# Moving the finishing of a head's output from VectorE to ScalarE and GpSimd (layer 1), and the splitting of the negated maximum from VectorE to GpSimd (layers 2 and 3)

## What is computed

```
# layer 1
dots = jnp.einsum('bhid,bhjd->bhij', q, k) * scale
attn = jax.nn.softmax(dots, axis=-1)
out = jnp.einsum('bhij,bhjd->bhid', attn, v)
out = out.transpose(0, 2, 1, 3).reshape(b, n, h * d)
return out @ Wo + bo
# layers 2 and 3
attn = jnp.einsum('bhqd,bhkd->bhqk', q, k) * SCALE
attn = jax.nn.softmax(attn, axis=-1)
out = jnp.einsum('bhqk,bhkd->bhqd', attn, v)
```

## Time and profile before

| | |
|---|---|
| median of 3 runs | 5328.83 us (5327.84 to 5330.45) |
| the profiled execution | 5331.11 us, of which the span of the trace is 5329.4 us |
| layer 1's attention in the trace | about 390 to 2880 us |
| layer 2's and layer 3's attention | about 3062 to 4100 us, 4255 to 5296 us |
| busy over the span | PE 92%, DVE 86%, ACT 58%, POOL 29% |

### The profile page before, as it was taken

The page is one execution under the profiler, slowest core; times in us unless marked ns, Lnnn a source line. Parts: engine busy times, 40 slices in busy tenths (PEclk is TensorE's granted clock), DMA queues, the critical chain, the costliest instruction groups (busy, mean ns, idle before and its releaser), DMA issues. The chain is left out here.

```text
span 5329.4 us, 73754 instructions
## 1 busy us (share of the span) xinstructions
PE 4899.8 (92%) x26357; PEld 1887.1 (35%) x26366; DVE 4600.4 (86%) x4742; ACT 3093.5 (58%) x6047; POOL 1543.5 (29%) x1202
## 2 busy tenths in 40 slices
PE   8938999999999999999997599999998699999997
PEld 5623454544445454444543222222222322222222
DVE  7649989899898989989895699999996499999996
ACT  3313444444444444444443288888886188888885
POOL 0014656565565656556564100000000100000000
PEclk9968999999999999999998699999998699999998
DMA  0024334232333423233220211111110211111110
GB/s 36 5 93 111 95 85 116 57 113 54 96 88 88 111 61 114 57 90 85 57 50 15 71 28 32 31 28 28 34 23 3 72 27 34 29 28 33 30 23 6
DMA packets 171366, 298.03 MB, mean 56 GB/s; under 512 B 39060, under 2 KB 108576, under 8 KB 167392
## 3 DMA queue, kind: packets, MB, share of 16 engines
q1 hardware_dynamic: 169420, 292.95, 21.8%
q10 hardware_dynamic: 1584, 0.37, 0.0%
HBM read 187.39 MB, written 101.25 MB: 54 GB/s over the span
## 5 line engine op out<-in xcount | busy, mean ns | idle before, releaser
L1777 DVE TENSOR_REDUCE a_mx<-ps 128x1 f32<-128x1024 f32 x1536 | 1814.5, 1220 | 72.5 <-PE ps L1611 56.4
L1719 ACT ACTIVATE a_prob<-ps 128x512 f32<-128x512 f32 (+1 forms) x3264 | 1699.4, 602 | 295.8 <-PE ps L1599 290.9
L1067 ACT ACTIVATE prob<-ps 128x512 f32<-128x512 f32 (+1 forms) x1888 | 974.8, 603 | 1183.1 <-PE ps L952 1178.7
L1170 POOL TENSOR_TENSOR tot_p<-tot_p,prob 128x512 f32<-128x512 f32 (+1 forms) x896 | 1341.5, 1497 | 915.7 <-ACT prob L1067 851.0
L1095 DVE TENSOR_REDUCE mx<-ps 128x1 f32<-128x1024 f32 x896 | 1051.3, 1215 | 152.2 <-PE ps L929 144.6
L1611 PE MATMUL ps<-a_K,a_Q 59*128 59x512 bf16 (+1 forms) x3328 | 1094.3, 386 | 57.4 <-DMA a_Q<-q_stack_dram 45.3
L1118 DVE TENSOR_TENSOR tot_d<-tot_d,prob 128x512 f32<-128x512 f32 x928 | 1051.9, 1134 | 88.0 <-ACT prob L1067 36.3
L1599 PE MATMUL ps<-a_Q,a_K 59*128 59x512 bf16 (+1 forms) x3264 | 991.2, 384 | 55.1 <-ACT a_prob L1719 48.9
L963 PE MATMUL ps<-prob,V 128*64 128x512 f32 x3776 | 929.4, 605 | 0.0
L1635 PE MATMUL ps<-a_prob,a_V 128*9 128x512 f32 x6528 | 873.9, 597 | 10.9 <-ACT a_acc L1703 10.9
L951 PE MATMUL ps<-QA,KA 128*128 128x512 f32 (+1 forms) x1888 | 805.9, 427 | 0.0
(11 more groups left out here) (405 smaller groups left out, 2968.1 us busy)
## 6 DMA issues: line engine op xcount, KB each, us to landing
a_K<-k_stack_dram SPq DMA_DIRECT2D x128, 300.2 KB
k_hi_dram<-hi_s SPq DMA_DIRECT2D x112, 256.0 KB
k_lo_dram<-lo_s SPq DMA_DIRECT2D x112, 256.0 KB
KA<-k_hi_dram SPq DMA_DIRECT2D x64, 384.0 KB, 4.3
KA<-k_lo_dram SPq DMA_DIRECT2D x64, 384.0 KB, 5.6
KB<-k_hi_dram SPq DMA_DIRECT2D x64, 384.0 KB, 6.5
k_bf_dram<-bf_s SPq DMA_DIRECT2D x112, 128.0 KB
KM<-k_bf_dram SPq DMA_DIRECT2D x32, 448.0 KB, 7.1
```

Of the source, the lines that this page charges most:

```text
L1067: nc.scalar.activation(prob[0:r, batch % 2, t % BATCH, :], c.banks(n % 3)[0:r, :], ACT.Exp, scale=SCALE).then_inc(exped, 1)
L1170: nc.gpsimd.tensor_tensor(tot_p[0:r, u % 2, :], tot_p[0:r, u % 2, :], p, ALU.add).then_inc(totalled_p, 1)
L1719: nc.scalar.activation(prob[0:r, batch % 2, t % BATCH, :], c.banks(n % 3)[0:r, :], ACT.Exp, scale=SCALE).then_inc(exped, 1)
L1777: nc.vector.tensor_reduce(mx[:, u % 2, j, i % FULL:i % FULL + 1], c.banks(slot(step), 2), AX.X, ALU.max).then_inc(maxed, 1)
```

## The change

Layer 1: ACT, behind the four exponentials of batch 1, copies the sums (to `den`) and the 128x512 product (to `fin_s`) out of PSUM; the second copy frees the slot, so a "fin" slot is now counted under `v_out`. DVE keeps only the reciprocal, from `den`. POOL, behind its two sums of batch 1, multiplies `fin_s` by the reciprocals and adds it to `c.y`, two instructions of 128x512. To make room, `gain` and `shift` are given back after the norm. Layers 2 and 3: DVE keeps the reduce to the negated maximum; POOL does the cast and the subtraction.

```diff
-        by_act, count = kind == "v", [0, 0] if not freed else list(freed[-1])
+        by_act, count = kind in ("v", "fin"), [0, 0] if not freed else list(freed[-1])
...
+                def take_fin(u):
+                    n = slot_no["fin", u]
+                    act.wait_ge(slotted, n + 1)
+                    if u >= 1:
+                        act.wait_ge(added, 2 * u)
+                        act.wait_ge(rec_ready, u)
+                    nc.scalar.copy(den[:], c.banks(slot(n) + 1)[:, 0:UQ]).then_inc(fin_out, 1)
+                    nc.scalar.copy(fin_s[:], c.banks(slot(n))).then_inc(v_out, 1)
...
-                def finish(u):
-                    n = slot_no["fin", u]
-                    dve.wait_ge(slotted, n + 1)
-                    inv, f = rec[:, u % 2, :], u % HALVES
-                    link(nc.vector.reciprocal(inv, c.banks(slot(n) + 1)[:, 0:UQ]))
-                    for j in range(UQ):
-                        y = c.y[:, UQ * f + j, :]
-                        last = nc.vector.scalar_tensor_tensor(out=y, in0=c.banks(slot(n))[:, j * P:(j + 1) * P],
-                                                              scalar=inv[:, j:j + 1], in1=y, op0=ALU.mult, op1=ALU.add)
-                    last.then_inc(released, 1)
+                def invert(u):
+                    dve.wait_ge(fin_out, u + 1)
+                    if u >= 2:
+                        dve.wait_ge(added, 2 * (u - 1))
+                    nc.vector.reciprocal(rec[:, u % 2, :], den[:]).then_inc(rec_ready, 1)
...
+                def add_up(u):
+                    pool.wait_ge(rec_ready, u + 1)
+                    pool.wait_ge(v_out, freed[slot_no["fin", u]][1])
+                    if u >= 2:
+                        pool.wait_ge(added, 2 * (u - 1))
+                    y = c.y[:, UQ * (u % HALVES):UQ * (u % HALVES + 1), :]
+                    share = fin_s[:].rearrange("p (j d) -> p j d", j=UQ)
+                    nc.gpsimd.tensor_tensor(share, share, rec[:, u % 2, :].unsqueeze(2).to_broadcast([P, UQ, D]),
+                                            ALU.mult).then_inc(added, 1)
+                    pool.wait_ge(added, 2 * u + 1)
+                    nc.gpsimd.tensor_tensor(y, y, share, ALU.add).then_inc(added, 1)
...
+            @block.gpsimd
+            def _(pool):
+                for u in range(UNITS):
+                    both, hi, lo = nm[:, u % 2, :], nmp[:, u % 2, :, 0], nmp[:, u % 2, :, 1]
+                    pool.wait_ge(nm_max, u + 1)
+                    if u >= 2:
+                        pool.wait_ge(scored, nm_no(u - 2) + 1)
+                    nc.gpsimd.tensor_copy(hi, both).then_inc(nm_cut, 1)
+                    pool.wait_ge(nm_cut, u + 1)
+                    nc.gpsimd.tensor_tensor(lo, both, hi, ALU.subtract).then_inc(nm_ready, 1)
...
-                        dve.wait_ge(scored, nm_no(u - 2) + 1)
-                    link(nc.vector.tensor_reduce(nm[:, u % 2, :], mx[:, u % 2, :, :], AX.X, ALU.max, negate=True))
-                    link(nc.vector.tensor_copy(nmp[:, u % 2, :, 0], nm[:, u % 2, :]))
-                    nc.vector.tensor_tensor(nmp[:, u % 2, :, 1], nm[:, u % 2, :], nmp[:, u % 2, :, 0], ALU.subtract
-                                            ).then_inc(nm_ready, 1)
+                        dve.wait_ge(nm_ready, u - 1)
+                    nc.vector.tensor_reduce(nm[:, u % 2, :], mx[:, u % 2, :, :], AX.X, ALU.max, negate=True
+                                            ).then_inc(nm_max, 1)
```

More of the change, by code:

```diff
@@ L739, in l1_attention @@
         sb = lambda n, s, d=FP32: c.sb(n, s, d, held)
-        gain, shift, bo = sb("gain", [P, D]), sb("shift", [P, D]), sb("bo1", [P, D])
+        bo = sb("bo1", [P, D])
         weights = [sb(f"weights{i}", [P, 4, P]) for i in range(2)]
@@ L755, in l1_attention @@
         nm, rec = sb("nm1", [P, 2, UQ]), sb("rec1", [P, 2, UQ])
[L756 to L782, removed]
@@ L783, in l1_attention, with _ @@
-        norm(c, gain, shift)
+        with ExitStack() as early:
+            gain, shift = (c.sb(n, [P, D], FP32, early) for n in ("gain", "shift"))
+            with phase(nc, "loaded") as (block, loaded):
+                @block.sync
+                def _(sp):
+                    sp.dma_start(gain[:], w["ln_g"].partition_broadcast(P)).then_inc(loaded, 16)
+                    sp.dma_start(shift[:], w["ln_b"].partition_broadcast(P)).then_inc(loaded, 16)
+                    sp.dma_start(bo[:], w["bo"].partition_broadcast(P)).then_inc(loaded, 16)
+                    for base in (0, DH):
+                        sp.dma_start(Wo_twice[0][base:base + DH, :], w["Wo"][0:DH, :]).then_inc(loaded, 16)
+                    sp.wait_ge(loaded, 16 * 9)
+                @block.scalar
+                def _(act):
+                    act.dma_start(weights[0][:, W_Q, :], w["Wq"][:, 0:P]).then_inc(loaded, 16)
+                    act.dma_start(weights[0][:, W_K, :], w["Wkv"][:, 0:P]).then_inc(loaded, 16)
+                    act.dma_start(weights[0][:, W_V, :], w["Wkv"][:, HEADS * DH:HEADS * DH + P]).then_inc(loaded, 16)
+                    act.dma_start(weights[0][:, W_M, :], w["Wm"][:, 0:P]).then_inc(loaded, 16)
+                @block.vector
+                def _(dve):
+                    nc.vector.memset(ones_col[:], 1.0)
+                    nc.vector.memset(V[:, TILES - 1, :], 0.0)
+                    for tile in QB:
+                        nc.vector.memset(f32(tile[DH:P, :]), 0.0)
+                @block.gpsimd
+                def _(pool):
+                    nc.gpsimd.memset(f32(KB[DH:P, :]), 1.0)
+            norm(c, gain, shift)
@@ L1073, in _ @@
                             take_v(*what)
+                        if kind == "fin":
+                            take_fin(what)
                         if b == NM_AT and u + 1 < UNITS:
@@ L1078, in _ @@
                 take_acc(UNITS - 1)
+                take_fin(UNITS - 1)
             @block.vector
@@ L1148, in _ @@
                         if kind == "fin":
-                            finish(what)
-                finish(UNITS - 1)
+                            invert(what)
+                invert(UNITS - 1)
             @block.gpsimd
@@ L1185, in _ @@
                             cast(what)
+                        if kind == "fin":
+                            add_up(what)
+                add_up(UNITS - 1)
         with phase(nc, "chain", "unused") as (block, chain, _):
```

16 lines of the change are left out of this document (10 added, 6 removed).

## The result

The changed kernel took 5302.11 us (median of 5 runs, 5298.47 to 5304.35), the kernel before 5327.84 (5 runs, 5325.39 to 5330.45): a ratio of 0.9951, with a 95% interval of 0.9936 to 0.9965. It is faster by 25.7 us. The prediction was 5297, in a range of 5290 to 5312.

The account below looks back on a forecast made before the run. Layer 1 was taken as held up by PE waiting for DVE's finishing adds, layers 2 and 3 as paced by PE, three score banks and ACT. -33.6 + 2.3 - 0.4 = -31.7 us gave 5297.1 us, range 5290 to 5312.

Parts of the forecast that it names:

- The wait in layer 1: Layer 1: PE's wait for the finishing slot in 23 places goes, with 0.6 us from seven other units; 33.6 us gained.
- The sum: Whole kernel: -33.6 + 2.3 - 0.4 = -31.7 us, giving a median of 5297.1 us.
- DVE may run 1.4 us later against PE than it does before PE notices.: Layer 1, plain batch: PE's second pair needs its slot about 909.3, DVE freed it at 907.93, so there is room.
- the return of nothing: Layer 1: none of the time gained in batch 1 is given back later in the unit; taken as nothing.
- POOL's added work: Layer 1: two more POOL instructions, 2.6 us a unit, cost nothing as POOL has time and hardly meets DVE's sums.
- Rival (b): Layer 1: POOL holds up DVE and PE waits for DVE later; 18 us come back, 5315 us; chance 0.07.
- The tail: End of layer 1: the last finishing, with nothing to hide it, takes 3.7 us instead of 1.4; +2.3 us.
- Layers 2 and 3: Layers 2 and 3: 62 of 64 units gain nothing; only the filling of each layer gains, 0.4 us for both together.
- rival (d): Layers 2 and 3: POOL's small instructions late; from 2.1 us on every us costs 62 us, 5353 at 3; chance 0.04.
- DVE runs beside it with a little to spare: Layers 2 and 3: PE, three score banks and ACT set the pace; DVE is outside that loop with slight room.
- The forecast's own range: Whole kernel, rivals left out: 26 to 33 us gained, 5296 to 5303 us; the forecast's chance 0.80.

Follow-up runs that it names:

- experiments 4 and 5: Kernel before; in 4 DVE does layer 1's finishing ahead of its two sums, 5317.51 us; in 5 ACT copies the slot out, DVE adds from the copy, 5320.64 us.
- experiment 9: Layer 1's half of the change, ACT copying and POOL adding, but the slot freed only by DVE's reciprocal behind its two sums: 5302.49 us, ratio 0.9951.
- experiment 1: Only layer 1's half of the change, layers 2 and 3 as in the kernel before: 5297.34 us, ratio 0.9946.
- experiment 6: Layer 1's half of the change alone, with POOL adding the share once more and taking it off again in each finishing: 5316.09 us, ratio 0.998.
- experiment 3: Kernel before, with DVE doing the cast and subtraction of the negated maximum twice in layers 2 and 3: 5356.82 us, ratio 1.0057.
- experiment 10: Layer 1's half of the change, with only the last unit finished by DVE from PSUM as before: 5299.5 us, ratio 0.9945.
- experiment 11: The whole changed kernel measured once more on the same chip: 5304.48 us, ratio 0.995.
- Experiment 2: Kernel before with only the half in layers 2 and 3, the split on POOL, layer 1 untouched: 5327.62 us, ratio 1.0001.

## Why the prediction was right, and where it was not

**The wait in layer 1 (-33.6).** The mechanism was right. Layer 1 became 31.3 us shorter. The sum had 1.43 us for each of 23 places; batch 1 of a unit got shorter by 1.46 to 1.48 in 14 of them, by 1.37 to 1.39 in three and by 1.13 in six (units 3, 7, 19, 23, 27 and 29). With the seven places that open a pair of heads, which gave 0.08 each, as predicted, that is 32.0 us of 33.6. In those six, and only there, DVE's opening copy was held up by POOL, as the last section shows; DVE's maxima of batch 1 then start 0.24 us later, and so do PE's finishing products, which wait for the slot that the first of them frees. Another 0.08 us came back in batch 4 of the seven units 1, 5, ..., 25, where PE waits for L1102, 0.6 in all.

**"DVE may run 1.4 us later against PE than it does before PE notices."** This step failed. It was read off one plain batch, where PE's second pair needs a slot freed a batch earlier. It holds for batches like that one and for those of unit 3, and not for all plain ones: late in units 2, 6 and so on DVE is 1.4 us later already, and under 0.5 us is left. A batch with a projection of kind "k" asks for one slot more, and there the room is close to nothing: with DVE 1.4 us later against PE, in experiments 4 and 5, 1.40 to 1.47 us came back in batch 4 wherever that batch has such a projection. So the reason given for the return of nothing was wrong in part, and that nothing came back but 0.6 us was partly luck. What keeps the gain is the other half of the same argument, the 1.3 us less that DVE has to do. The four cases, by medians against the kernel before measured beside each:

| | DVE adds | POOL adds |
|---|---|---|
| slot freed behind DVE's sums | 0 | -25.7 (experiment 9) |
| slot freed early | -9, -7 (experiments 4, 5) | -29 (experiment 1) |

The early slot with DVE's adds kept, and its sums a little longer, gives a quarter to a third. DVE without the adds gives nearly everything, but that isn't the lighter load by itself: in experiment 9 the slot still comes only after the sums, and yet about 1.1 us earlier, since the adds no longer stand between them and PE. What the four show is that an early slot pays in full only if DVE is also relieved, and that ACT's freeing adds 3.4 us by the traces to what the relief gives; the medians of experiments 1 and 9 don't tell them apart. For a change that freed the slot early and did no more, the same working would have promised some 33 us where 7 to 9 were measured.

**POOL's added work (0).** Right in size. The sum's mean fell by 10 ns instead of growing, and PE has no wait for POOL. Rival (b), which expected 18 us back, did not occur, but its mechanism exists: experiment 6, with another pair of the same instructions, lost 19 us. The margin was below one more pair, and the prediction didn't know it.

**The tail (+2.3).** It measured +2.2: 8.56 us from the last exponential to the bias before, 10.77 after. The working had two errors that cancel. From PE's end to the end of the last add it was 3.2 us and not 3.7 (2845.72 to 2848.92), though the sum had left out DVE's reciprocal, so 1.8 us more than before; the other 0.4 came between the last add and the bias, 0.9 us before and 1.3 after, which the sum didn't have.

**Layers 2 and 3 (-0.4).** Right. A unit stands at 31.56 us in both traces. Each filling gained 0.14 us, together 0.3. The parts were ready in 0.54 us where 0.9 was taken, and rival (d) was far off; its threshold of 2.1 us was confirmed as 1.98. The idle time ahead of the turning's weight load grew from 0.23 us to 0.61: the maximum product's load ahead of it is earlier, and the turning, which waits for ACT, is not. "DVE runs beside it with a little to spare" was right in sign, and experiment 3 put the little at 0.11 us or less. DVE's waits for PE in layer 2 rose from 16.8 us in 61 places to 24.5 in 87, 7.7 us in 30 units or 0.26 us a unit, where 0.4 was expected.

**The sum.** By the parts that the change touches, -31.3 + 2.2 - 0.3 = -29.4 us, against -31.7 predicted and -29 for layer 1's half by median. The whole change showed -25.7 and, repeated, -23.7, but the intervals of all three overlap. The forecast's own range, 5296 to 5303, holds the first median and not the second, and as a gain, 26 to 33 us, it misses both, the first by 0.3 us. One thing that moves a single execution by such an amount is TensorE's clock in the last unit of layer 3. Windows of the changed kernel there (stretch, its us, busy us of PE, PEld, DVE, ACT, POOL, granted clock, DMA share, GB/s):

```profile
5234.00:5238.00 4.00, 2.12 (x13) 0.67 (x12) 2.86 (x5) 1.65 (x4) 0.00 (x0) 0.86 0.00 0
5238.00:5242.00 4.00, 4.00 (x16) 0.41 (x14) 3.82 (x6) 1.57 (x3) 0.00 (x0) 0.50 0.00 0
5242.00:5246.00 4.00, 4.00 (x14) 0.86 (x10) 3.86 (x5) 1.00 (x2) 0.00 (x0) 0.50 0.00 0
```

and of experiment 10 at the same place of the program:

```profile
5236.00:5240.00 4.00, 3.22 (x20) 0.81 (x22) 3.82 (x6) 1.85 (x5) 0.00 (x0) 1.00 0.00 0
```

After 4 us in which PE was busy for 2.12, the clock stood at 0.50, its lower level of 1.2 GHz, for some 12 us in the changed kernel. It did so in the profiled execution of before too, and in experiment 11, so the clock doesn't explain the gain. In experiment 10 it stayed at 1.00, and in 1 it fell only in part. Layer 3 took 1019.65 us in the changed kernel, 1019.75 before, 1019.66 in experiment 11, 1015.15 in 1 and 1014.6 in 10. Experiment 2, which has POOL's split, took 1015.6, and experiments 4 and 5, which don't have it, fell to 0.50 and took 1018.4 and 1018.1; so the split doesn't force the fall, and the fall doesn't need it. Whether the split makes it likelier was not tried, and one profile of each kernel can't tell. Against the kernel before beside each, the whole change gained 3 to 5 us less than layer 1's half (23.7 and 25.7 against 29); that stays open.

## What to carry to other kernels

When PE waits for a slot, there are two debts: when the slot is freed, and how much work the freeing engine has until PE meets it again. Paying only the first here moved most of the wait to the next places where PE takes an extra slot, so a return of nothing must be shown for every kind of batch, not for a plain one. A table of two by two (slot early or late, engine heavy or light) helps, if one checks in the traces that each kernel moves only what its name says; taking the adds away here also moved the slot. And in layers 2 and 3, where DVE had 0.11 us of room or less, relief gave nothing and a burden cost nearly its full price: test both directions before calling an engine idle.

## What the hardware showed that was not expected

DVE's copy of 128x512 that opens each sum takes 0.42 us in some units, 0.58 in others and 1.52 in a few. It is 0.42 or 1.52 where the copy and POOL's two-input sum start almost together. The changed kernel, where POOL's L1180 starts 0.03 us ahead:

```profile
972.67 1.27 POOL L1180 TENSOR_TENSOR tot_p<-tot_p,prob 128x512 f32<-128x512 f32 x1
972.70 1.52 DVE L1130 COPY tot_d<-prob 128x512 f32<-128x512 f32 x1
```

The kernel before, where the same two start 0.02 us apart and POOL's is the longer one:

```profile
978.37 1.55 POOL L1170 TENSOR_TENSOR tot_p<-tot_p,prob 128x512 f32<-128x512 f32 x1
978.39 0.41 DVE L1115 COPY tot_d<-prob 128x512 f32<-128x512 f32 x1
```

In the first the copy ends at 974.22, 0.28 us behind POOL's instruction; in the second POOL's is stretched from 1.27 to 1.55 and the copy is as short as anywhere. The Trainium skill (SBUF — State Buffer, Who interferes with whom) lists copies among the DVE instructions that can take the pair of ports shared with GpSimd and has whoever issues first keep it for the whole instruction. The trace agrees in that one of the two is held up (1.52 - 0.41 = 1.11 us, and 1.55 - 1.27 = 0.28). It doesn't show who issued first: in both cases POOL's record starts first.

What separates the two is a few nanoseconds. Such a meeting comes in nine units of each trace, 117 times in the thirteen. The copy was short in 51 of them, where it starts 10 to 22 ns behind POOL's sum (once 24), and long in 66, at 21 to 26 ns. None was long in the kernel before, five in each of experiments 2 and 3 with the same layer 1, six in the changed kernel, eight in experiment 11, the changed kernel again. Where the slot is freed early, a long copy costs PE time without exception: in the nine traces of this kind batch 1 took 6.26 to 6.28 us in the 25 places with a short copy, and 6.50 to 6.52 (in unit 11 up to 6.87) in the 56 with a long one. No experiment forced the copy one way or the other, but the two never came apart.

POOL's product with a broadcast reciprocal took 1.04 us for 128x512 and its addition 1.29. Small instructions were cheaper than the nearest rows had suggested: ACT's copy of 128x4 0.16 us (taken: at most 0.35), POOL's cast and subtraction of 128x4 0.19 and 0.20 (taken: 0.25).
